# Local transformer layer norm: statistics from token rows on VectorE instead of from features by TensorE

## The chip, the cores and the metric

One core of a Trainium2 chip. The metric is the device time of one execution in microseconds (us), the median of several runs. TensorE does the matmuls and transposes, VectorE, ScalarE and GpSimd the rest, SyncE issues the transfers. In the rows PE is TensorE, PEld its weight loads, DVE is VectorE, ACT is ScalarE, POOL is GpSimd.

## What is computed

Input x is 16 batch rows of 512 tokens by 128 features. The reference, cut:

```python
xn = _layernorm(x)
x = x + _L0_attn_ref(xn, ...) + _L0_ffn_ref(xn, ...)

# _L0_attn_ref: causal attention, 16 heads of 64, with biases
# _L0_ffn_ref: two layers (DEPTH = 2), each:
h = shift_token(x)                       # half of the features come from the token before
q, k, v = jnp.split(h @ wqkv, 3, axis=-1)
q = l2norm(q) * qs; k = l2norm(k) * ksc  # 8 heads of 64
q, k = rotary_xpos(q, k)
x = x + local_attention(q, k, v) @ wo    # windows of 64 tokens, the window before is seen too
h = shift_token(x)
mu = h.mean(-1, keepdims=True); var = h.var(-1, keepdims=True)
h = (h - mu) / jnp.sqrt(var + 1e-05) * lg + lb
a, g = jnp.split(h @ w1 + b1, 2, axis=-1)
x = x + (a * gelu(g)) @ w2 + b2
```

The last formulas, from `mu` to `lb`, and the final sum of the three terms are what the change touches.

## The kernel before

**Work and streams.** All in float32. A batch row passes through 182 steps, each a task such as `("f_wo", l)`: a group of TensorE instructions that fill one or more of 8 PSUM banks, and the instructions on ScalarE or VectorE (sometimes GpSimd too) that read the banks. Steps that begin with `a_` belong to the attention (8 pairs of heads: `a_proj`, `a_v`, `a_max`, `a_neg`, `a_st`, `a_pv`, `a_ot`, `a_out`), steps with `f_` to the local transformer, with the layer (0 or 1) as their first number. A layer has a front (`f_q`, `f_k`, `f_v`, and the transposes `f_qt`, `f_kt`, for 4 token tiles; GpSimd normalises q and k), four rounds of local attention (`f_max`, `f_neg`, `f_st`, `f_pv`, `f_ot`), and a tail: `f_wo`, the layer norm, `f_gate`, three `f_up`, `f_down`. `norm` and `f_first` bring in a batch row, `xt` makes the attention's copy of it, `out` adds everything up and stores.

**What sets the order.** At build time a planner (`least_idle`, L249) walks through four streams at once: layer 0 with `norm` and `f_first`, layer 1, the attention's front, and the attention's rest. It gives every step the costs that stand in the table `STEPS` (L64 to L97), observes the dependences in `needs` (L145) and the 8 banks, keeps the 40 best partial orders after every step, and ranks them by TensorE's idle time in that model plus a penalty when the streams drift apart. The result, `ORDER` (L288), is one list, and every engine works through its own instructions in the order of that list, with semaphore waits for what it needs. So a change of costs in the table moves steps everywhere. Layer 1 of batch row i runs beside layer 0 of batch row i + 1.

**Dependences that matter here.** `f_first` of a batch row needs `f_down` of layer 0 of the row before, `xt` needs `f_first`, and the attention's projections need `xt`; `f_down` of layer 0 needs `f_wo` of layer 1 of the row before; the last `a_out` of a batch row needs `out` of the row before.

**The layer norm before** (features on partitions, tokens along the free axis) takes three steps:
- `f_mean` (L1241, L830): one 128x512 matmul with the matrix `center` subtracts each token's mean; ScalarE copies the result (`centred`) and squares it (`squared`).
- `f_var` (L1245, L984, L703): four matmuls of `squared` with `mean_of` give each token's variance; VectorE adds epsilon (`lvar`), GpSimd takes the power -0.5 (`lrstd`).
- `f_rep` (L1250, L988, L836): four matmuls repeat `lrstd` over the partitions; VectorE scales (`scaled`), ScalarE adds the bias into `lT`, which `f_gate` and `f_up` read.

**The final sum before:** `out` (L1273, L1035) adds `aT` (attention) and `yT` (local transformer) by eight accumulating matmuls with the identity, which also turn them to token rows, and VectorE adds x.

The input norm at the start of each batch row, `token_norm` (L863), works on token rows in SBUF: four `bn_stats`, four `bn_aggr`, an add of epsilon, GpSimd's power, four `tensor_scalar`.

## Time and profile before

| | us |
|---|---|
| median of 3 runs (3051.53 to 3061.63) | 3054.31 |
| span of the profiled execution | 3052.9 |
| TensorE busy | 2932.4 |
| VectorE busy | 1987.4 |
| ScalarE busy | 1704.3 |
| GpSimd busy | 1019.2 |

The profiled execution shows its span, from the first to the last instruction; what lies around the span is not shown separately, and the span is 1.4 us below the median. Busy time counts an engine's instructions; matmuls overlap each other, so a matmul's own duration is longer than the time to the start of the next. A float32 matmul stands as two records, a transpose as one. An idle time in square brackets in a timeline is that of the engine just ahead of the row, with what released it.

### The profile page before, as it was taken

The page shows a single profiled execution, that of the slowest core. Times are in us where ns is not written, and L with a number is a line of the kernel's source. Part 1 is how long each engine was busy: PE and PEld are TensorE (multiplying, and loading weights), DVE is VectorE, ACT ScalarE, POOL GpSimd, SP SyncE. Part 2 cuts the span into 40 slices and gives each one's busy share as a digit, 9 for nine tenths or more (in the row PEclk, how much of TensorE's full clock was granted, in tenths as well). Part 3 has the DMA queues.
Part 4 walks back from the last instruction along what each step waited for, and adds up shares of the span by engine and source line. Part 5 has one row for each costly group of instructions (what it writes and reads, how often), then busy time and mean ns, then how long its engine had stood idle before and what let it go on. Part 6 is the DMA issues. An engine that isn't in the chain of part 4 may idle for free.

```text
span 3052.9 us, 86127 instructions
## 1 busy us (share of the span) xinstructions
PE 2932.4 (96%) x33792; PEld 2004.3 (66%) x33792; DVE 1987.4 (65%) x6942; ACT 1704.3 (56%) x3094; POOL 1019.2 (33%) x1002
## 2 busy tenths in 40 slices
PE   6999999999999999999999999999999999999997
PEld 4666666676666666666666766666667676666764
DVE  5567676666767566676767666676675766666653
ACT  4455464655555565555556655566565655655552
POOL 5134250424324052352414324152250423423230
PEclk9999999999999999999999999999999999999998
DMA  3000000000000000000000000000000000000000
GB/s 102 2 5 2 10 4 2 12 2 12 2 4 10 2 12 2 9 5 2 12 2 9 5 9 5 2 9 5 8 5 2 12 2 8 5 2 9 2 8 5
DMA packets 41783, 25.03 MB, mean 8 GB/s; under 512 B 13058, under 2 KB 40620, under 8 KB 41388
## 3 DMA queue, kind: packets, MB, share of 16 engines
q1 hardware_dynamic: 41388, 19.52, 2.3%
q8 instruction: 277, 4.54, 0.6%
q14 instruction: 118, 0.97, 0.1%
HBM read 14.96 MB, written 4.19 MB: 6 GB/s over the span
## 4 chain that ended last, share of the span: by engine, by line
PE 83%; DVE 7%; ACT 4%; issue 4%; POOL 2%; DMA 0%; POOLq 0%; DVEq 0%; ACTq 0%
PE bank L1139 10%; PE bank L1182 9%; PE bank L1168 7%; PE bank L1056 7%; PE bank L1223 6%; PE bank L1195 4%; PE bank L1239 4%; PE bank L1208 3%; PE bank L1228 3%; PE bank L1049 3%; PE bank L1261 3%; PE bank L1266 3%; PE bank L1050 3%; PE bank L1051 3%; PE bank L1271 2%
## 5 line engine op out<-in xcount | busy, mean ns | idle before, releaser
L910 DVE CUSTOM_DVE_ANT_0 bank<-bank,future 128x128 f32<-128x128 f32 (+3 forms) x1024 | 467.3, 527 | 68.8 <-PE bank L1098 68.2
L925 DVE CUSTOM_DVE_ANT_0 bank<-bank,band 128x192 f32<-128x192 f32 x1024 | 331.0, 394 | 226.1 <-PE bank L1116 225.7
L714 POOL TENSOR_TENSOR rnorm<-ssc,minus_half 128x8 f32<-128x8 f32 x256 | 426.8, 1667 | 21.3
L780 ACT ACTIVATE probs<-bank 128x512 f32<-128x512 f32 (+1 forms) x768 | 346.0, 532 | 143.7 <-PE bank L1148 143.1
L712 POOL TENSOR_SCALAR ssc<-ss 128x8 f32<-128x8 f32 x256 | 99.7, 390 | 934.4 <-DVE ss L970 930.4
L1139 PE MATMUL bank<-Qa,Ka 64*128 64x512 f32 (+3 forms) x2048 | 391.3, 465 | 8.0 <-ACT lprobs L787 4.4
L1182 PEld LDWEIGHTS bank<-Va,probs 128*64 128x64 f32 x10240 | 312.4, 138 | 47.3 <-issue 38.3
L1182 PE MATMUL bank<-Va,probs 128*64 128x65 f32 x10240 | 332.6, 223 | 0.0
L963 DVE TENSOR_TENSOR scratch<-bank,rope_t 128x512 f32<-128x512 f32 x256 | 176.2, 688 | 230.0 <-ACT scratch L807 207.9
L807 ACT ACTIVATE scratch<-bank 128x512 f32<-128x512 f32 x256 | 153.8, 601 | 259.9 <-PE bank L1223 167.5
L787 ACT ACTIVATE lprobs<-bank 128x512 f32<-128x512 f32 x256 | 139.0, 595 | 283.0 <-PE bank L1170 282.9
L1223 PE MATMUL bank<-Lqkv,resid 128*128 128x512 f32 x512 | 272.9, 618 | 4.1 <-ACT resid L800 2.1
L702 POOL TENSOR_TENSOR rstd<-var_eps,minus_half 128x4 f32<-128x4 f32 x16 | 16.1, 1009 | 778.1 <-DVE var_eps L875 778.1
L1168 PE MATMUL bank<-Qf,Kf 64*128 64x64 f32 x4096 | 254.8, 275 | 0.0
L1168 PEld LDWEIGHTS bank<-Qf,Kf 64*128 64x128 f32 x4096 | 240.3, 189 | 15.0
L733 ACT ACTIVATE Qf<-bank 128x512 f32<-128x512 f32 x256 | 152.9, 604 | 91.5 <-PE bank L1056 91.4
L1139 PEld LDWEIGHTS bank<-Qa,Ka 64*128 64x128 f32 x2048 | 158.9, 188 | 37.9 <-issue 26.5
L1195 PEld LDWEIGHTS bank<-V_shifted,lprobs 128*64 128x64 f32 x2048 | 137.0, 138 | 62.8 <-issue 38.1
L970 DVE TENSOR_REDUCE ss<-scratch 128x8 f32<-128x512 f32 x256 | 172.6, 674 | 0.0
L1195 PE MATMUL bank<-V_shifted,lprobs 128*64 128x65 f32 x2048 | 167.3, 228 | 1.0 <-ACT lprobs L787 0.8
L1195 PE MATMUL bank<-Vf,lprobs 128*64 128x65 f32 x2048 | 167.4, 228 | 0.0
L718 POOL TENSOR_TENSOR scratch<-scratch 128x512 f32<-128x512 f32 x128 | 162.8, 1272 | 0.0
(164 smaller groups left out, 6496.5 us busy)
## 6 DMA issues: line engine op xcount, KB each, us to landing
x_res<-in_L_attn_x SPq DMA_DIRECT2D x16, 256.0 KB, 2.9
x_rows<-in_L_attn_x SPq DMA_DIRECT2D x16, 256.0 KB, 3.2
out<-yT SPq DMA_DIRECT2D x16, 256.0 KB, 2.5
Lqkv<-in_L_ffn_wqkv SPq DMA_DIRECT2D x2, 768.0 KB, 4.8
rope_t<-in_rope SPq DMA_DIRECT2D x8, 128.0 KB, 4.7
Kf<-in_L_attn_W_qkv SPq DMA_DIRECT2D x1, 768.0 KB, 7.4
Qf<-in_L_attn_W_qkv SPq DMA_DIRECT2D x1, 768.0 KB, 9.0
Lw<-in_L_ffn_w SPq DMA_DIRECT2D x2, 341.0 KB
```

The costliest lines, as they stand in the source:

```text
L714: g.tensor_tensor(rnorm[s][:, :], ssc[:, :], minus_half[:, :], ALU.pow).then_inc(rnorm_ready.sem, 1)
L780: psum.raise_read(a.activation(probs[j][:, at:at + n], psum.bank(i, task, (u, j))[:, 0:n], ACT.Exp, scale=float(HEAD) ** -0.5), i, task, ( ...
L910: ins = v.tensor_tensor_reduce(psum.bank(i, task, (u, j))[:, at:at + n], psum.bank(i, task, (u, j))[:, at:at + n], future[:, SEQ - n:SEQ], ...
L925: ins = v.tensor_tensor_reduce(psum.bank(i, task, (u, j))[:, k * BAND:(k + 1) * BAND], psum.bank(i, task, (u, j))[:, k * BAND:(k + 1) * BAND],
L963: v.tensor_tensor(heads(turn_a), src, table(0, 0, HEAD), ALU.mult)
L970: v.tensor_reduce(ss[s][:, :], heads(squares), AX.X, ALU.add).then_inc(sums_ready.sem, 1)
L1056: ins = nc.tensor.transpose(bank[:, t * P:(t + 1) * P], src(t), ident[:, :])
L1139: mm(bank[j][:, at:end], Ka[p % 2][HALF[j], tile(k)], Qa[p % 2][HALF[j], queries], start=True, stop=False)
L1168: mm(bank[j][:, queries], K_padded[l][HALF[j], keys], Qf[l][HALF[j], p, queries], start=False, stop=False)
L1182: ins = mm(bank[part, t * (HEAD + 1):(t + 1) * (HEAD + 1)], probs[j][:, at + part.start:at + part.stop], Va[p // 2 % 2][:, k, 2 * (p % 2) ...
L1195: ins = mm(bank[HALF[b % 2], t * (HEAD + 1):(t + 1) * (HEAD + 1)], lprobs[j][:, b * BLOCK:(b + 1) * BLOCK], V[:, t, 2 * p + j, :], start=T ...
L1223: psum.raise_filled(mm(bank[:, :], resid[l][:, tile(t)], Lqkv[l][:, c * INNER:(c + 1) * INNER], start=True, stop=True), i, task, kind[2])
```

## The change

The layer norm is done on token rows. `f_rows` replaces `f_mean` and `f_var`: four TensorE transposes turn the residual (`resid`) into token rows in a bank; VectorE takes `bn_stats`, `bn_aggr` and the add of epsilon, waits for GpSimd's power, and writes centred and scaled rows into `lrows` (part of the buffer `ff`). `f_back` replaces `f_rep`: four transposes turn the rows back, and ScalarE applies gain and bias in one instruction into `lT`. In `out`, VectorE first adds `aT` to `yT`, then TensorE does four transposes in place of eight matmuls. The planner gets new costs, and the constants `center` and `mean_of` go.

```diff
-    "f_var": [("pe", 0.9, (), (0,), ()), ("dve", 0.15, (0,), (), (0,)), ("pool", 0.95, (1,), (), ())],
+    "f_rows": [("pe", 0.46, (), (0,), ()), ("dve", 2.05, (0,), (), ()), ("pool", 1.0, (1,), (), ()), ("dve", 1.4, (2,), (), (0,))],
+    "f_back": [("pe", 0.46, (), (0,), ()), ("act", 0.8, (0,), (), (0,))],
...
@@ -165,7 +164,7 @@
         if at[1]:
             return [(i, ("f_k", at[0], at[1] - 1), 0)]
...
-                elif kind == "f_mean":
-                    j0, t0 = earlier(i, task, lambda t: t[0] == "f_up" and t[2] == LAST_UP)
-                    psum.wait_read(act, j0, t0, "a")
-                    psum.wait_filled(act, i, task, "c")
-                    a.activation(centred, psum.bank(i, task, "c")[:, :], ACT.Copy)
-                    psum.raise_read(a.activation(squared, psum.bank(i, task, "c")[:, :], ACT.Square), i, task, "c")
-                elif kind == "f_rep":
+                elif kind == "f_back":
                     l = task[1]
                     if i == 0:
                         act.wait_ge(params, PARAMS)
                     j0, t0 = earlier(i, task, lambda t: t[0] == "f_up" and t[2] == LAST_UP)
                     psum.wait_filled(act, j0, t0, "a")
-                    psum.wait_read(act, i, task, "r")
-                    a.activation(lT[:, :], scaled, ACT.Identity, bias=lnb[:, l:l + 1]).then_inc(lt_ready.sem, 1)
+                    alone(i, task, "h", lT[:, :], psum.bank(i, task, "h")[:, :], ACT.Identity, scale=lng[:, l:l + 1], bias=lnb[:, l:l + 1])
...
+            def token_stats(i, task, mark):
+
+                bank = tiles_of(psum.bank(i, task, mark)[:, :])
+                j0, t0 = earlier(i, task, lambda t: t[0] == "f_rows")
+                psum.wait_read(dve, j0, t0, "c")
+                psum.wait_filled(dve, i, task, mark)
+                for t in range(TILES):
+                    ins = v.bn_stats(lstats[:, t, :], bank[:, t, :])
+                ins.then_inc(rows_ready.sem, 1)
+                rows_ready.wait(dve, i, task, "s")
+                for t in range(TILES):
+                    ins = v.bn_aggr(lmv[:, t, :], lstats[:, t, :])
+                ins.then_inc(rows_ready.sem, 1)
+                rows_ready.wait(dve, i, task, "a")
+                v.tensor_scalar(lvar[:, :], lmv[:, :, 1], EPS, None, ALU.add).then_inc(rows_ready.sem, 1)
+                j0, t0 = earlier(i, task, lambda t: t[0] == "f_back")
+                psum.wait_filled(dve, j0, t0, "h")
+                rstd_ready.wait(dve, i, task, "p")
+                for t in range(TILES):
+                    ins = v.tensor_scalar(lrows[:, t, :], bank[:, t, :], lmv[:, t, 0:1], lrstd[:, t:t + 1],
+                                          ALU.subtract, ALU.mult)
+                psum.raise_read(ins, i, task, mark)
...
-                elif kind == "f_var":
-                    psum.wait_filled(dve, i, task, "v")
-                    psum.raise_read(v.tensor_scalar(
-                        lvar[:, :], psum.bank(i, task, "v")[:, 0:2 * TILES].rearrange("p (t n) -> p t n", n=2)[:, :, 0],
-                        EPS, None, ALU.add), i, task, "v")
-                elif kind == "f_rep":
-                    l = task[1]
-                    if i == 0:
-                        dve.wait_ge(params, PARAMS)
-                    psum.wait_read(dve, i, ("f_mean", l), "c")
-                    psum.wait_filled(dve, i, task, "r")
-                    psum.raise_read(v.scalar_tensor_tensor(scaled, centred, lng[:, l:l + 1], psum.bank(i, task, "r")[:, :],
-                                                           ALU.mult, ALU.mult), i, task, "r")
+                elif kind == "f_rows":
+                    token_stats(i, task, "c")
...
-                        if p == PAIRS - 1:
-                            psum.wait_filled(dve, before_it(i, task, ("out",)), ("out",), "t")
...
+                    other = ("a_out", PAIRS - 1)
+                    psum.wait_read(dve, before_it(i, task, other), other, "u")
+                    other = ("f_down", DEPTH - 1)
+                    psum.wait_read(dve, i, other, "w")
+                    v.tensor_tensor(yT[:, :], yT[:, :], aT, ALU.add).then_inc(sum_ready.sem, 1)
...
-                elif kind == "f_mean":
+                elif kind == "f_rows":
                     l = task[1]
-                    bank = psum.claim(pe, i, task, "c", [(("f_wo", l), "w")])
-                    psum.raise_filled(mm(bank[:, :], center[:, :], resid[2 * l][:, 0:SEQ], start=True, stop=True), i, task, "c")
-                elif kind == "f_var":
-                    bank = psum.claim(pe, i, task, "v", [(("f_mean", task[1]), "c")])
-                    for t in range(TILES):
-                        ins = mm(bank[:, 2 * t:2 * t + 2], squared[:, tile(t)], mean_of[:, :], start=True, stop=True)
-                    psum.raise_filled(ins, i, task, "v")
-                elif kind == "f_rep":
-                    rstd_ready.wait(pe, i, ("f_var", task[1]), "p")
-                    bank = psum.claim(pe, i, task, "r")
-                    for t in range(TILES):
-                        ins = mm(bank[:, tile(t)], lrstd[:, t:t + 1].broadcast_to([P, P]), ident[:, :], start=True, stop=True)
-                    psum.raise_filled(ins, i, task, "r")
+                    transposes(i, task, "c", lambda t: resid[2 * l][:, tile(t)], [(("f_wo", l), "w")])
+                elif kind == "f_back":
+                    transposes(i, task, "h", lambda t: lrows[:, t, :], [(("f_rows", task[1]), "c")])
...
-                    lt_ready.wait(pe, i, ("f_rep", l), "h")
                     for j, (c, m) in enumerate(HID_CHUNKS):
-                        bank = psum.claim(pe, i, task, j)
+                        bank = psum.claim(pe, i, task, j, [(("f_back", l), "h")])
...
-                    other = ("a_out", PAIRS - 1)
-                    psum.wait_read(pe, before_it(i, task, other), other, "u")
-                    bank = psum.claim(pe, i, task, "t", [(("f_down", DEPTH - 1), "w")])
-                    for t in range(TILES):
-                        mm(bank[:, tile(t)], aT[:, tile(t)], ident[:, :], start=True, stop=False)
-                        ins = mm(bank[:, tile(t)], yT[:, tile(t)], ident[:, :], start=False, stop=True)
-                    psum.raise_filled(ins, i, task, "t")
+                    sum_ready.wait(pe, i, task, "y")
+                    transposes(i, task, "t", lambda t: yT[:, tile(t)])
```

**How the order moves: TensorE, layer 1 of the eighth batch row, from its f_wo on.** `Qf,Lwo` is `f_wo`, `GLU,Lw` is `f_down` of layer 0 of the next batch row, `resid,center` is `f_mean`, `Wqkv` is `a_proj` or `a_v` of the attention, `identb,neg` is `a_neg`. Before:

```order
L1239 MATMUL bank<-Qf,Lwo 128x512 x4
L1271 MATMUL bank<-GLU,Lw 128x512 x3
L1244 MATMUL bank<-resid,center 128x512
L1049 MATMUL bank<-Wqkv_hi,xT_hi 128x256
L1050 MATMUL bank<-Wqkv_hi,xT_lo 128x256
L1051 MATMUL bank<-Wqkv_lo,xT_hi 128x256
L1049 MATMUL bank<-Wqkv_hi,xT_hi 128x256
L1050 MATMUL bank<-Wqkv_hi,xT_lo 128x256
L1051 MATMUL bank<-Wqkv_lo,xT_hi 128x256
L1126 MATMUL bank<-identb,neg 128x128 x4
```

Of the change, from the last `f_ot` of layer 1 on (`ident,resid` is `f_rows`, `ident,ff` is `f_back`, L1255 `f_gate`, L1260 `f_up`, `ident,x_res` is `f_first` and then `xt`):

```order
L1061 MATMUL bank<-ident,Of 128x128 x4
L1244 MATMUL bank<-Qf,Lwo 128x512 x4
L1265 MATMUL bank<-GLU,Lw 128x512 x3
L1061 MATMUL bank<-ident,resid 128x128 x4
L1061 MATMUL bank<-ident,ff 128x128 x4
L1255 MATMUL bank<-lT,Lw 128x512 x2
L1255 MATMUL bank<-lT,Lw 85x512
L1260 MATMUL bank<-lT,Lw 128x512
L1061 MATMUL bank<-ident,x_res 128x128 x4
L1260 MATMUL bank<-lT,Lw 128x512
L1061 MATMUL bank<-ident,x_res 128x128 x4
L1228 MATMUL bank<-Lqkv,resid 128x512 x2
```

Before, 13 rows of attention stood between `f_mean` and `f_var`, of which 7 are shown; now `f_rows` and `f_back` stand next to each other. Such a pair, `ident,resid` with `ident,ff` right behind it, stands at 15 of the 32 layer norms of the changed program: layer 1 of every batch row but the third. In 14 of them `f_wo` and `f_down` stand right ahead as here, in the last batch row `f_wo` alone. In 12 of the batch rows before the last, the twelve steps from `f_st` of the third round to `f_wo` have nothing of another stream among them either; in the program before, the last batch row alone was so. From the seventh batch row on the order of the change repeats itself, up to the last two.

**VectorE at the same place.** Before (L980 and L981 are `f_wo`, L1016 and L1017 `f_down`, then `norm` of a later batch row, L985 `f_var`, L994 `f_rep`):

```order
L980 TENSOR_TENSOR resid<-bank,resid 64x512
L981 TENSOR_TENSOR resid<-bank,resid 64x512
L1016 SCALAR_TENSOR_TENSOR resid<-bank,b2s,resid 64x512
L1017 SCALAR_TENSOR_TENSOR resid<-bank,b2s,resid 64x512
L868 BN_STATS stats<-x_res 128x6 x4
L872 BN_AGGR mv<-stats 128x2 x4
L875 TENSOR_SCALAR var_eps<-mv 128x4
L878 TENSOR_SCALAR x_res<-x_res,mv,rstd 128x128 x4
L985 TENSOR_SCALAR lvar<-bank 128x4
L994 SCALAR_TENSOR_TENSOR ff<-ff,lng,bank 128x512
```

Of the change (L993 and L994 are `f_wo`, L1018 and L1019 `f_down`, L879 to L891 `f_rows`):

```order
L993 TENSOR_TENSOR resid<-bank,resid 64x512
L994 TENSOR_TENSOR resid<-bank,resid 64x512
L1018 SCALAR_TENSOR_TENSOR resid<-bank,b2s,resid 64x512
L1019 SCALAR_TENSOR_TENSOR resid<-bank,b2s,resid 64x512
L879 BN_STATS lstats<-bank 128x6 x4
L883 BN_AGGR lmv<-lstats 128x2 x4
L886 TENSOR_SCALAR lvar<-lmv 128x4
L891 TENSOR_SCALAR ff<-bank,lmv,lrstd 128x128 x4
L858 BN_STATS stats<-x_res 128x6 x4
L862 BN_AGGR mv<-stats 128x2 x4
L865 TENSOR_SCALAR var_eps<-mv 128x4
L868 TENSOR_SCALAR x_res<-x_res,mv,rstd 128x128 x4
```

The four rows of `f_rows` come behind the adds of `f_wo` and `f_down`, and `norm` behind them.

**TensorE behind the out of the last batch row but one.** Before, layer 1 of the last batch row begins so (`Lqkv` is `f_q`, `f_k` or `f_v`; `qn` and `kn` are `f_qt` and `f_kt`; L1208, L1098 and L1182 are attention):

```order
L1223 MATMUL bank<-Lqkv,resid 128x512
L1098 MATMUL bank<-Ka,Qa 128x128 x2
L1098 MATMUL bank<-Ka,Qa 128x256 x2
L1098 MATMUL bank<-Ka,Qa 128x384 x2
L1098 MATMUL bank<-Ka,Qa 128x512 x2
L1182 MATMUL bank<-Va,probs 64x65 x20
L1228 MATMUL bank<-Lqkv,resid 128x512
L1223 MATMUL bank<-Lqkv,resid 128x512
L1056 MATMUL bank<-ident,qn 128x128 x4
L1223 MATMUL bank<-Lqkv,resid 128x512
L1182 MATMUL bank<-Va,probs 64x65 x20
L1056 MATMUL bank<-ident,kn 128x128 x4
```

Of the change (`ident,yT` is `out`, L1213 the last `a_out`):

```order
L1260 MATMUL bank<-lT,Lw 128x512 x2
L1260 MATMUL bank<-lT,Lw 85x512
L1265 MATMUL bank<-GLU,Lw 128x512 x3
L1061 MATMUL bank<-ident,yT 128x128 x4
L1213 MATMUL bank<-OaT,Wout 128x512
L1228 MATMUL bank<-Lqkv,resid 128x512 x2
L1233 MATMUL bank<-Lqkv,resid 128x512
L1228 MATMUL bank<-Lqkv,resid 128x512
L1061 MATMUL bank<-ident,qn 128x128 x4
L1228 MATMUL bank<-Lqkv,resid 128x512
L1061 MATMUL bank<-ident,kn 128x128 x4
L1233 MATMUL bank<-Lqkv,resid 128x512
```

The attention of the last batch row is over before this layer begins, and the rest of the program has rows of layer 1 alone; before, the attention ran beside it up to the second round.

## Rows read from the trace of the kernel before

**Rows 1.** Page, part 1: busy time of each engine
```profile
PE 2932.4 (96%) x33792; PEld 2004.3 (66%) x33792; DVE 1987.4 (65%) x6942; ACT 1704.3 (56%) x3094; POOL 1019.2 (33%) x1002
```

**Rows 2.** Windows: middle and last stretch; busy us (x instructions) per engine, PEclk, DMA share, GB/s
```profile
200.00:2800.00 2600.00, 2537.16 (x29320) 1733.59 (x29319) 1736.35 (x6059) 1486.09 (x2697) 903.65 (x853) 1.00 0.02 6
...
2950.00:3053.00 103.00, 81.99 (x886) 53.80 (x882) 45.50 (x152) 37.88 (x70) 24.24 (x23) 0.90 0.01 4
```

**Rows 3.** TensorE timeline, one layer norm in mid-run: start us, us, engine line op
```profile
1237.92 1.02 PE L1244 MATMUL bank<-resid,center 128*128 128x512 f32 x2
1238.87 1.13 PE L1139 MATMUL bank<-Qa,Ka 64*128 64x512 f32 x4
...
1242.17 1.05 PE L1248 MATMUL bank<-mean_of,ff 128*128 128x2 f32 x8
1243.08 0.63 PE L1056 MATMUL bank<-ident,Oa 128*128 128x128 f32 x4
...
1244.32 0.66 PE L1056 MATMUL bank<-ident,x_res 128*128 128x128 f32 x4
1244.81 1.02 PE L1208 MATMUL bank<-OaT,Wout 128*128 128x512 f32 x2
1245.67 1.05 PE L1254 MATMUL bank<-ident,lrstd 128*128 128x128 f32 x8
1246.56 1.88 PE L1223 MATMUL bank<-Lqkv,resid 128*128 128x512 f32 x4
```

**Rows 4.** TensorE timeline, final step out of the last batch row
```profile
3047.62 0.39 PE L1279 MATMUL bank<-ident,yT 128*128 128x128 f32 x2
...
3048.96 0.39 PE L1279 MATMUL bank<-ident,yT 128*128 128x128 f32 x2
```

**Rows 5.** Timeline of VectorE and GpSimd: f_down, norm and f_var in one stretch
```profile
2712.67 0.74 DVE L1016 SCALAR_TENSOR_TENSOR resid<-bank,b2s,resid 64x512 f32<-64x512 f32 x1 [1.25 <-PE bank L1271]
...
2714.22 0.87 DVE L868 BATCH_NORM_STATS2 stats<-x_res 128x6 f32<-128x128 f32 x4
...
2715.79 1.02 POOL L702 TENSOR_TENSOR rstd<-var_eps,minus_half 128x4 f32<-128x4 f32 x1 [56.72 <-DVE var_eps L875]
...
2716.85 1.11 DVE L878 TENSOR_SCALAR x_res<-x_res,mv,rstd 128x128 f32<-128x128 f32 x4 [1.13 <-POOL rstd L702]
...
2717.99 0.16 DVE L985 TENSOR_SCALAR lvar<-bank 128x4 f32<-128x4 f32 x1
```

**Rows 6.** TensorE timeline, end of layer 1 of the last batch row
```profile
3011.10 0.38 PE L1126 MATMUL bank<-identb,negf 128*128 128x128 bf16 x4 [1.52 <-issue]
...
3015.43 0.27 PE L1195 MATMUL bank<-V_shifted,lprobs 128*64 128x65 f32 x1 [0.16 <-ACT lprobs L787]
...
3017.67 0.65 PE L1056 MATMUL bank<-ident,Of 128*128 128x128 f32 x4 [1.07 <-DVE Of L944]
3019.01 3.70 PE L1239 MATMUL bank<-Qf,Lwo 128*128 128x512 f32 x8 [0.69 <-ACT Qf L733]
```

**Rows 7.** TensorE timeline, a_proj, the row behind it, and both a_pv
```profile
1852.11 0.48 PE L1049 MATMUL bank<-xT_hi,Wqkv_hi 128*128 128x512 f32 x1
...
1853.59 1.02 PE L1208 MATMUL bank<-OaT,Wout 128*128 128x512 f32 x2
...
1856.28 2.55 PE L1182 MATMUL bank<-Va,probs 128*64 128x65 f32 x80
```

**Rows 8.** GpSimd timeline, one q and k pair of a front
```profile
1267.14 0.54 POOL L712 TENSOR_SCALAR ssc<-ss 128x8 f32<-128x8 f32 x1 [6.57 <-DVE ss L970]
...
1274.04 1.04 POOL L723 TENSOR_TENSOR kn<-scratch,rnorm 128x512 f32<-128x512 f32 x1 [0.17 <-POOL scratch L718]
```

**Rows 9.** TensorE timeline: one wait of TensorE in mid-run
```profile
1863.46 0.38 PE L1126 MATMUL bank<-identb,neg 128*128 128x128 bf16 x4 [2.46 <-DVE neg L910]
```

**Rows 10.** Windows behind that wait and behind one in the first batch row
```profile
1865.20:1868.60 3.40, 3.40 (x24) 1.73 (x21) 1.00 (x2) 1.08 (x2) 3.21 (x3) 0.50 0.26 77
...
124.40:131.20 6.80, 6.80 (x71) 5.83 (x70) 0.77 (x3) 1.59 (x3) 0.00 (x0) 0.50 0.01 2
```

38 lines of the change are left out of this document (17 added, 21 removed).

## The prediction

> **What bounds the kernel now.** I read the busy times first, then windows, then the waits of TensorE in a timeline. TensorE is busy for 2932.4 of 3052.9 us, VectorE for 65% [rows 1]. In the 2600 us of the middle TensorE is busy for 2537.2 us and its clock stays at full rate [rows 2]: 62.8 us idle, or 4.3 us in each batch row of some 178 us (2600 us hold 14.6 of them). So before the change TensorE's own work sets the time, and the order hides nearly every dependence behind another stream's work. Only where one stream runs alone do the waits show: the last 103 us hold 21.0 us of idle time and a mean clock of 0.90 [rows 2].
>
> So there are two questions: how much work TensorE loses, and whether the new order still hides the chain through VectorE, GpSimd and ScalarE. The second one decides, and it can be read from the order.
>
> **A. TensorE's work: -77 us.** What a step occupies is the time from its start to the next step's start when nothing waits. `f_mean` takes 1238.87 - 1237.92 = 0.95 us, `f_var` 0.91, `f_rep` 0.89, four transposes 0.49 (1244.32 to 1244.81) [rows 3]. A layer norm took 2.75 us and takes 2 x 0.49 = 0.98: 1.77 us less, 32 times, 56.6 us. In `out`, the records of one kind start 0.22 us apart, from 3047.62 to 3048.96 in six steps [rows 4], so its eight matmuls take 8 x 0.22 = 1.79 us; four transposes take 0.49. That is 1.3 us less, 16 times, 20.8 us. Sum 77.4 us, 4.8 us in each batch row. If everything else stayed hidden, this would be the gain.
>
> **B. The hole between f_rows and f_back: +77 us.** In the new order these two stand next to each other on TensorE in layer 1 of 15 batch rows, in 14 of them right behind `f_wo` and `f_down`. TensorE works in order, so it stands still until VectorE has written the rows. VectorE at that time has to add `f_down` and then do the whole of `f_rows`. The parts stand in a row in the trace: from the first add of `f_down`, which starts when its matmuls end, over the input norm with its `bn_stats`, its wait for GpSimd's 1.02 us and its four `tensor_scalar`, from 2712.67 to 2716.85 + 1.11 = 2717.96, 5.29 us; the norm alone takes 3.74 (2714.22 to 2717.96) [rows 5]. `f_rows` is the same instructions on the same shapes, read from a bank in place of SBUF. The adds of `f_wo` run under the matmuls of `f_down`. Of the 5.29 us TensorE covers 0.49 with the transposes of `f_rows`; 4.8 us stay. Then `f_gate` needs the rows turned back: transposes, one 128x512 read by ScalarE, a matmul. The same form stands between the last `f_ot` and `f_wo`, and TensorE waited 0.69 us there [rows 6]. So 4.8 + 0.7 = 5.5 us, 14 times, 77 us. Behind that `norm` stands on VectorE (3.7 us) and `f_first` waits for it, but `f_back`, that wait, `f_gate` and an `f_up` lie between on TensorE, and these are more than 3.7 us. Below: the hole can be no shorter than VectorE's own 3.74 us less 0.49, which gives 4.0 with the 0.7, so 55 us; above: 0.5 us more if reading a bank is slower, 84 us.
>
> **C. Bare rounds ahead of it: +41 us.** In 12 batch rows the last two rounds of layer 1 have no other stream's steps among them. The last batch row ran the same twelve steps bare already before the change, and TensorE waited there 1.52 us ahead of `f_neg`, 0.16 ahead of `f_pv`, 1.07 ahead of `f_ot`, 0.69 ahead of `f_wo` [rows 6]: 3.44 us, 12 times, 41 us.
>
> **D. The clock: +24 us.** The clock fell to half rate, 1.2 GHz, for 3.4 us right behind a wait of 2.46 us in mid-run [rows 9, 10], and for 6.8 us behind waits in the first batch row [rows 10]. TensorE was busy throughout in both stretches, so they cost half: 1.7 and 3.4 us. A hole of 4.8 us, with the 0.7 behind it, is more than twice the wait that brought one on. I take the shorter stretch, since part of it passes in the hole itself: 14 x 1.7 = 24 us. The ends are none and 14 x 3.4 = 48 us. The Trainium skill (TensorE: Matmul & The Clock Gate, section PE-mode transpose) has a rule that speaks against this change: transposes do not count as work for the clock as matmuls do, and all that is left of the layer norm on TensorE is transposes, on both sides of the hole. By that rule the longer stretch would be the common one, and the sum 24 us higher. No row here shows transposes alone, so the sum stays with the mid-run row.
>
> **E. The end of the program: +26 us.** The attention of the last batch row is now over before its layer 1 begins. Its front then goes at the pace of GpSimd: a q and k pair takes 1267.14 to 1275.08, 7.94 us [rows 8], four pairs 31.8 us. TensorE has 12 matmuls of 0.94 (half of 1.88) and 8 transposes of 0.49 in it [rows 3], 15.2 us, so 16.6 us idle. Entering and leaving that stretch through ScalarE and VectorE I put at 4 us, with 0 and 8 as ends. Two more rounds are bare, 2 x 3.4. The `out` ahead of it waits for two adds of `f_down` and one of the sum on VectorE, about 3 us more than it did. Against this, some 5 of the 21.0 us of idle time at the end [rows 2] lay in the mixed stretch that is gone. 16.6 + 4 + 6.9 + 3 - 5 = 26 us. The very last layer norm has a shorter chain than its three steps had, and the last `out` a longer one; I put both together at nothing.
>
> **F. Edits that cost nothing.** In layer 0, `f_rows` and `f_back` have other work between them: two transposes steps (`a_ot`, `f_kt`), one `a_proj` of 1.48 us (1852.11 to 1853.59), both `a_pv` 2.55 [rows 7], one `a_out` 0.86 [rows 3], together 5.9 us against the 3.74 that VectorE needs. Without that cover it would be B once more. VectorE gains some 90 us of work over the whole run (3.74 less the wait for GpSimd and less the one small and one 128x512 instruction removed, 32 times, and 16 adds); it is at 65%, and this sits in its idle time except where B counts it. ScalarE loses instructions. The small idle time of mid-run stays, but the tenth of it that lay where B and C now are goes: -6 us.
>
> **Sum.** -77 + 77 + 41 + 24 + 26 - 6 = +85. The profiled span of 3052.9 becomes 3138, and with the 1.4 us by which the median lies above it, **3139 us, 2.8% slower**.
>
> **The rivals.**
> 1. *The bound engine's saving comes through*, 3054 - 77 = **2977 us**. For it: TensorE is at 96%, a whole batch row of other work exists, and the three old steps waited on each other too and hardly showed. Against it: the order of the change. Its one point of decision is the exposed time in a batch row, which has to stay below the 4.8 us saved; B and C give 5.5 + 3.4. Chance 0.08. The Trainium skill (Perfetto Trace Analysis, section Identifying the Most-Contended Engine) says to optimize the engine with the highest occupancy first, and this is what comes out by that rule.
> 2. *VectorE held up by GpSimd in layer 0.* The power for `lrstd` stands in GpSimd's queue behind the q and k work, and VectorE now waits for it with everything behind. The cover has 5.9 - 3.7 = 2.2 us to spare; half a pair (4 us [rows 8]) ahead of it would expose about 2 us, and the stopped VectorE would delay the reads of `a_pv`. 16 times 2.3 us, **3176 us**. Against it: three more steps of attention stand between the last `f_k` and `f_rows`. Chance 0.12.
> 3. *Half of B and C is hidden and the clock stays up*, because the new order is tighter elsewhere and mid-run idle time halves: 3139 - 59 - 24 = 3056, or less by up to 31 us: around **3050 us**. Against it: TensorE issues in order, so nothing later can fill the hole. Chance 0.08.
>
> My forecast keeps 0.72. **The numbers.** About 0.3%, 9 us, is what a measurement of this kernel can tell from no change. Faster takes rival 1 and a third of rival 3: 0.10; the same, half of rival 3: 0.04; slower, the rest: 0.86. Below, the range takes the forecast without the clock's cost and with mid-run idle time halved, 3139 - 24 - 31 = 3084; above, the longer clock stretches, 3163, and rival 2 with most of them, 3190.
>
> **What would show it.** Right: TensorE's busy time falls, and its busy share falls from 96% to about 90%; in each batch row a wait of nearly 5 us ahead of the transposes of `ff` (L1061), released by VectorE's `tensor_scalar` (L891); windows at half clock right behind it; a front of layer 1 at the end that takes over 30 us with GpSimd busy throughout; 15 layer norms of the 32 with a hole. Wrong: if those transposes wait less than 2 us, B fails and rival 1 is near; if the clock never falls in mid-run, D; if waits gather ahead of the layer 0 `f_back`, rival 2.

## The result and the profile after

| | before | change |
|---|---|---|
| median, us | 3052.92 | 3285.98 |
| lowest to highest, us | 3050.92 to 3061.63 | 3284.43 to 3287.63 |
| span of the profiled execution, us | 3052.9 | 3282.6 |

The change is slower by a ratio of 1.0756 [1.0740, 1.0771]: 233 us where the forecast had 85, and outside its range. The direction was right, and the holes stand where the forecast put them, as the trace shows. The cost of the clock and idle time elsewhere were put far too low.

The page of the changed kernel, part 1, busy time of each engine:

```profile
PE 2964.1 (90%) x33280; PEld 1994.8 (61%) x33280; DVE 2065.6 (63%) x7310; ACT 1689.3 (51%) x3030; POOL 1019.3 (31%) x999
```

TensorE has 512 matmul records fewer than in [rows 1] and is busy for 31.7 us longer. The windows answer to those of [rows 2], and two are added: one steady batch row, and the two stretches of it at half clock (busy us and instructions of PE, PEld, DVE, ACT, POOL, then the clock):

```profile
200.00:2800.00 2600.00, 2386.74 (x27057) 1607.35 (x27056) 1677.95 (x5943) 1375.52 (x2470) 828.47 (x781) 0.97 0.02 6
...
1733.00:1934.40 201.40, 184.10 (x2080) 124.02 (x2079) 128.48 (x456) 105.57 (x189) 62.59 (x59) 0.97 0.02 6
...
1721.70:1728.40 6.70, 6.59 (x70) 5.54 (x67) 0.71 (x3) 1.58 (x3) 0.00 (x0) 0.50 0.00 0
1742.20:1748.90 6.70, 5.47 (x9) 2.43 (x10) 2.69 (x14) 2.96 (x4) 1.01 (x1) 0.50 0.00 1
...
3150.00:3283.00 133.00, 89.11 (x470) 51.32 (x470) 48.10 (x146) 33.65 (x54) 30.75 (x29) 0.65 0.02 7
```

In mid-run the clock is no longer 1.00. In the steady part it falls twice in every batch row, for some 6.8 us each time, and the last 133 us of the program have a mean clock of 0.65. Summed over the run, the clock stands at half rate, 1.2 GHz, for 272.8 us in 32 stretches, against 36.1 us in 6 before (both counts take in some 2 us behind the last instruction).

The waits of TensorE, grouped by what ended them (us in total, times, longest; `issue` means that the profile shows nothing it waited for), first of the change:

```profile
PE bank L1061 <- DVE ff L891: 81.1, 17, 5.7
PE bank L1131 <- issue: 25.8, 26, 2.5
PE bank L1255 <- ACT lT L729: 19.0, 29, 0.9
PE bank L1061 <- DVE yT L1040: 18.2, 14, 2.5
PE bank L1103 <- ACT Qa L729: 18.1, 11, 1.7
PE bank L1103 <- ACT probs L776: 15.0, 28, 0.7
...
PE bank L1144 <- ACT lprobs L783: 13.2, 12, 1.1
PE bank L1061 <- DVE Of L957: 12.6, 14, 1.1
```

and those of before that answer to them (L1056 was the transposes' line, L1126 that of `f_neg` and `a_neg`):

```profile
PE bank L1126 <- issue: 6.6, 13, 1.5
...
PE bank L1056 <- DVE Of L944: 4.4, 6, 1.1
PE bank L1139 <- ACT lprobs L787: 4.4, 4, 1.1
...
PE bank L1098 <- ACT probs L780: 3.1, 9, 0.5
...
PE bank L1261 <- ACT lT L843: 2.8, 4, 1.7
PE bank L1098 <- ACT Qa L733: 2.2, 2, 1.4
```

**Where 230 us of span come from.** TensorE's idle time rose from 120.5 to 318.5 us, by 198. Its busy time rose by 31.7 although its work at full clock fell by the 77 of term A, so some 109 us are left over for half clock. The records of the clock allow that: 272.8 - 36.1 = 236.7 us more at half rate cost at most half of that, 118. Then -77 + 198 + 109 = 230. What is left over takes in every other error, that of term A too. Read directly, half of the time that TensorE is busy inside the recorded stretches is 217.5 / 2 = 108.7 us of the change and 28.7 / 2 = 14.3 before, so 94 us more; the other 15 are not accounted for. By place, the 108.7 are 38 around the 14 holes of mid-run, 32 in ten stretches in the bare rounds, 31 from the `out` of the last batch row but one on (before: 7) and 7 elsewhere.

One steady batch row shows it too. It takes 201.4 us. Before, by an estimate, it took 2932.4 / 16 = 183.3 us of busy time at the busy share of mid-run, 0.976, so 187.8. Of the 13.6 us between them, -4.8 are saved work, 17.3 - 4.5 = +12.8 idle time, and the rest, +5.6, the clock; half of the busy time in its two stretches is (6.59 + 5.47) / 2 = 6.0.

The place is the one forecast. TensorE's timeline at the end of layer 1 of a batch row in mid-run (start, us, engine, line, then in brackets the wait ahead of it):

```profile
1720.04 0.38 PE L1131 MATMUL bank<-identb,negf 128*128 128x128 bf16 x4 [1.53 <-issue]
...
1721.43 3.45 PE L1173 MATMUL bank<-Qf,Kf 64*128 64x64 f32 x32
...
1729.10 0.66 PE L1061 MATMUL bank<-ident,Of 128*128 128x128 f32 x4 [0.81 <-DVE Of L957]
1730.44 3.70 PE L1244 MATMUL bank<-Qf,Lwo 128*128 128x512 f32 x8 [0.69 <-ACT Qf L729]
1733.98 2.74 PE L1265 MATMUL bank<-GLU,Lw 128*128 128x512 f32 x6
1736.56 0.60 PE L1061 MATMUL bank<-ident,resid 128*128 128x128 f32 x4
1742.50 1.11 PE L1061 MATMUL bank<-ident,ff 128*128 128x128 f32 x4 [5.34 <-DVE ff L891]
1744.54 2.93 PE L1255 MATMUL bank<-lT,Lw 128*128 128x512 f32 x3 [0.93 <-ACT lT L729]
```

and VectorE's timeline of the same hole:

```profile
1736.83 0.74 DVE L1018 SCALAR_TENSOR_TENSOR resid<-bank,b2s,resid 64x512 f32<-64x512 f32 x1 [1.25 <-PE bank L1265]
...
1741.08 1.37 DVE L891 TENSOR_SCALAR ff<-bank,lmv,lrstd 128x128 f32<-128x128 f32 x4 [1.19 <-POOL lrstd L701]
```

The hole of term B is there, 5.34 + 0.93 us, and so are the waits of term C, 1.53, 0.81 and 0.69. What the forecast had not seen is the second stretch at half clock: it begins at 1721.7, right behind the wait of 1.53 us, and the 32 matmuls of L1173 take 3.45 us, where a round at full clock took 1.98.

### The profile page after: what moved, and what is told of

It reads as the page before. It is cut to its first block, busy times and chain, and to the rows that moved or that the text cites. A ratio compares the mean times of both kernels' runs of the same rounds, so it can differ in the third digit from the quotient of the medians.

```text
span 3282.6 us, 85395 instructions
## 1 busy us (share of the span) xinstructions
PE 2964.1 (90%) x33280; PEld 1994.8 (61%) x33280; DVE 2065.6 (63%) x7310; ACT 1689.3 (51%) x3030; POOL 1019.3 (31%) x999
## 4 chain that ended last, share of the span: by engine, by line
PE 74%; DVE 11%; ACT 6%; issue 6%; POOL 2%; DMA 0%; ACTq 0%; DVEq 0%; POOLq 0%
PE bank L1187 9%; PE bank L1061 8%; PE bank L1144 8%; PE bank L1173 7%; PE bank L1228 6%; PE bank L1200 4%; PE bank L1213 3%; PE bank L1244 3%; PE bank L1255 3%; DVE bank L923 3%; PE bank L1233 3%; PE bank L1054 2%; PE bank L1131 2%; PE bank L1056 2%; PE bank L1055 2%
## 5 line engine op out<-in xcount | busy, mean ns | idle before, releaser
L1144 PE MATMUL bank<-Qa,Ka 64*128 64x512 f32 (+3 forms) x2048 | 389.5, 462 | 18.2 <-ACT lprobs L783 13.2
L701 POOL TENSOR_TENSOR lrstd<-lvar,minus_half 128x4 f32<-128x4 f32 x32 | 32.5, 1014 | 947.6 <-DVE lvar L886 947.5
L1228 PE MATMUL bank<-Lqkv,resid 128*128 128x512 f32 x512 | 279.5, 632 | 4.9 <-ACT resid L796 2.8
L1173 PE MATMUL bank<-Qf,Kf 64*128 64x64 f32 x4096 | 274.5, 288 | 0.0
L1173 PEld LDWEIGHTS bank<-Qf,Kf 64*128 64x128 f32 x4096 | 259.5, 202 | 15.9 <-issue 1.4
L1200 PE MATMUL bank<-V_shifted,lprobs 128*64 128x65 f32 x2048 | 176.7, 236 | 3.1 <-ACT lprobs L783 2.4
L1200 PE MATMUL bank<-Vf,lprobs 128*64 128x65 f32 x2048 | 177.0, 236 | 0.0
L1200 PEld LDWEIGHTS bank<-V_shifted,lprobs 128*64 128x64 f32 x2048 | 146.7, 146 | 47.6 <-issue 24.1
```

The costliest lines, as they stand in the source:

```text
L1144: mm(bank[j][:, at:end], Ka[p % 2][HALF[j], tile(k)], Qa[p % 2][HALF[j], queries], start=True, stop=False)
L1173: mm(bank[j][:, queries], K_padded[l][HALF[j], keys], Qf[l][HALF[j], p, queries], start=False, stop=False)
L1200: ins = mm(bank[HALF[b % 2], t * (HEAD + 1):(t + 1) * (HEAD + 1)], lprobs[j][:, b * BLOCK:(b + 1) * BLOCK], V[:, t, 2 * p + j, :], start=T ...
L1228: psum.raise_filled(mm(bank[:, :], resid[l][:, tile(t)], Lqkv[l][:, c * INNER:(c + 1) * INNER], start=True, stop=True), i, task, kind[2])
```

## The experiments

Two theories. **Order:** the edits by themselves save the 77 us, and the planner's new order, which leaves layer 1 bare, loses them and more. **Steps:** the new steps themselves put VectorE between two pieces of TensorE's work and are slower in any order. Beside them stands a question of size: how much is the clock, and how much the waits.

### The edits in the order of before

The planner is given the costs of before, and its finished order is then renamed:

```diff
+ORDER = [(i, ({"f_mean": "f_rows", "f_rep": "f_back"}.get(t[0], t[0]), *t[1:])) for i, t in ORDER if t[0] != "f_var"]
```

> All edits of the change, but every step stands in the order of the kernel before: f_rows in the place of f_mean, f_back in the place of f_rep, f_var left out. Theory 1, the new order is what costs (it leaves the chain of layer 1 bare): TensorE's saving of some 77 us comes through for the most part, 2975 to 3010 us. Theory 2, the new layer norm itself costs, since VectorE is held for 5 us in one piece and waits for GpSimd with everything behind it, in whatever order: 3070 to 3150 us, with waits for VectorE's rows at most of the 32 layer norms.

Measured: 3243.63 us, ratio 1.0603 [1.0582, 1.0623]. That is above the ranges of both theories. So the order of before doesn't carry the new steps either, and the theory of the order alone is wrong in its simple form. The waits of TensorE show why (L894 is the line of the scaled rows here, L1043 that of the sum in `out`):

```profile
PE bank L1064 <- DVE yT L1043: 65.9, 16, 7.3
PE bank L1057 <- DVE ff L894: 37.9, 8, 5.6
PE bank L1147 <- DVE ff L894: 22.6, 5, 5.5
PE bank L1106 <- DVE ff L894: 17.7, 5, 5.9
```

The sum in `out` costs 0.69 us on VectorE, yet TensorE waits up to 7.3 us for it. VectorE's timeline ahead of one of them:

```profile
1349.02 0.29 DVE L926 CUSTOM_DVE_ANT_0 bank<-bank,future 128x128 f32<-128x128 f32 x1
...
1354.43 0.69 DVE L991 TENSOR_TENSOR scratch<-scratch 128x512 f32<-128x512 f32 x1
1355.03 0.69 DVE L1043 TENSOR_TENSOR yT<-yT,aT 128x512 f32<-128x512 f32 x1
```

Instructions of other steps, without a gap from 1349.02 to 1355.03, stand ahead of the sum in VectorE's queue. Its own inputs had been ready since 1346.72 (1345.96 + 0.76). TensorE waited 5.27 us for it, up to 1355.77. In this order TensorE runs ahead of VectorE by those steps. With the old steps that hardly showed: TensorE was idle for 120.5 us in all, against 310.4 here.

### The steps of before in the order of the change

```diff
+ORDER = [(i, (kind, *t[1:])) for i, t in ORDER
+         for kind in {"f_rows": ("f_mean", "f_var"), "f_back": ("f_rep",)}.get(t[0], (t[0],))]
```

> The steps of the kernel before (old layer norm and old out, nothing of the change's edits), in the order that the planner made for the change: f_mean and f_var in the place of f_rows, f_rep in the place of f_back. Theory 1, the order costs: the holes stay, since the old chain has four waits of 1.2 to 1.7 us when nothing covers it (5.8 us in all, against 5.3 + 0.9 of the new one), and TensorE's 77 us of work come back: 3330 to 3370 us. Theory 2: the old steps do not mind the order, 3060 to 3150 us.

Measured: 3372.54 us, 1.1018 [1.0990, 1.1045], just above the range of the first theory. The order is bad for the old steps too, and as bad: TensorE is idle for 317.8 us (a span of 3372.8 less 3055.0 busy), against 318.5 with the new steps, and what differs is its busy time, by 90.9 us. In the order of the change the edits are thus worth 3372.54 - 3285.98 = 87 us in their favour, and in the order of before they cost 3243.63 - 3055.46 = 188 us. A price of the edits without an order does not exist.

### The hole filled with matmuls

Right ahead of `f_back`, where it follows `f_rows` directly, five matmuls are written into its bank, which the transposes then overwrite. They need nothing from VectorE, so the hole keeps its length but TensorE is not idle in it.

```diff
+                    bank = psum.claim(pe, i, task, "h")
+                    if PLACE[i, task] == PLACE[i, ("f_rows", task[1])] + 1:
+                        for _ in range(FILLERS):
+                            mm(bank[:, :], Wout[:, 0, :], resid[2 * task[1]][:, 0:SEQ], start=True, stop=True)
```

> The changed kernel with five extra 128x512 matmuls (results overwritten, the output stays as it is) ahead of f_back wherever it stands right behind f_rows, 4.7 us of work in a hole of 5.3. If half clock behind the hole costs about 2.5 us each time, as I now read the trace (6.8 us at half rate in each batch row there): 35 us less than the change, 3245 to 3260 us, and only one stretch at half clock in a batch row in mid-run. If the clock costs nothing there: 3286 to 3295 us.

Measured: 3242.19 us, 1.0597 [1.0572, 1.0621], 44 us less than the change. The wait for `ff` falls from 81.1 us to 16.0, since the fillers stand in it, and half clock falls from 272.8 us to 150.9 (20 stretches). TensorE does 75 matmuls more and the program is faster, so idle time in the hole does bring the clock down: around the 14 holes of mid-run the change had 14 stretches of 6.8 us, and here four of 3.4 us are left, each some 8 us behind the first filler of a hole.

The gain is not 44 / 15 at each hole, though. Out of the profiled execution (3246.8 us, the slowest of four), the stretch ahead of the hole and one whole batch row:

```profile
1706.90:1720.50 13.60, 12.10 (x72) 7.59 (x71) 1.21 (x4) 2.19 (x4) 0.00 (x0) 0.50 0.00 0
1523.00:1724.40 201.40, 188.55 (x2092) 125.61 (x2091) 128.54 (x457) 105.61 (x189) 62.58 (x59) 0.97 0.02 6
```

In four batch rows in a row the stretch that began in the bare rounds became twice as long, 13.7 us, and these rows take 201.4 us as they did unfilled. There the loss moved and did not go. Of the 38 us by which this execution's span is shorter than that of the change, none comes from these four rows, some 10 from the time behind the `out` of the last batch row but one, and the rest from the rows before and behind the four.

### The bare rounds filled too

The same, with one matmul more ahead of each `f_neg` of the last two rounds of layer 1 that has three steps of the local transformer right ahead of it, 15 in all. The expectation speaks of one ahead of `f_wo` too; the kernel that ran has none there.

```diff
+                    if kind == "f_neg" and task[1:] in ((1, 3), (1, 2)) and all(t[0][0] == "f" for _, t in ORDER[PLACE[i, task] - 3:PLACE[i, task]]):
+                        bank = psum.claim(pe, i, task, "m")
+                        mm(bank[:, :], Wout[:, 0, :], resid[2][:, 0:SEQ], start=True, stop=True)
```

> As fill_hole (3242 us), with one more 128x512 matmul ahead of the bare f_neg of the fourth round and a 128x256 one ahead of the f_wo behind it, in each batch row with bare rounds. The first stretch at half clock in a batch row (6.8 us, it slows f_st from 2.0 to 3.5 us) begins behind the wait of 1.5 us at that f_neg. If that wait alone sets it off: it goes in some 12 batch rows, 12 x 2 to 3 us, 3205 to 3220 us. If the waits behind it would bring it on as well: 3235 to 3250 us.

Measured: 3228.91 us, 1.0568 [1.0549, 1.0587]; 13 us less than with the hole alone filled, between the two ranges expected. Half clock falls to 85.8 us in 17 stretches. A steady batch row takes 197.9 us in place of 201.4, with one stretch of 3.4 us, which now begins at `f_wo`, behind the waits of 1.07 and 0.69 us that stayed unfilled. TensorE's waits elsewhere stay: 19.0 us for `lT`, 18.1 for `Qa`, 18.0 for `yT`. Together the fillers give back 57 us. The clock's loss itself, counted as above, falls by more, from 108.7 to 33.7 us. Part of what it gives back goes into longer waits (for `Of` 15.0 us in place of 12.6, for `lprobs` in `f_pv` 4.4 in place of 2.4); the rest is not traced.

### The order of before, with norm behind f_rows

In the order of before, `norm` stands ahead of `f_rows` of layer 1 and so ahead of it in VectorE's queue, with its wait for GpSimd. The two are exchanged:

```diff
+for k in range(1, len(ORDER) - 1):
+    if ORDER[k][1][0] == "norm" and ORDER[k + 1][1] == ("f_rows", 1):
+        ORDER[k], ORDER[k + 1] = ORDER[k + 1], ORDER[k]
```

> As new_in_old_order (3244 us), with one edit: where norm stands right ahead of f_rows of layer 1, the two change places, so that VectorE does the layer norm's rows before the next input's. Theory 3: in the old order the new layer norm is late because VectorE has 3.7 us of norm to do first (it hardly mattered for the old one, whose only VectorE work there was one 0.16 us instruction), so the waits for its rows (95 us in all there) lose about 3.5 us at each of 14 to 16 places: 3170 to 3200 us. If VectorE's queue is not the cause but the length of the chain itself: 3235 to 3250 us.

Measured: 3221.44 us, 1.0547 [1.0528, 1.0566]: 22 us less than without the exchange, between the two ranges expected. Waits of TensorE in this run (L1046 is the sum in `out`, L874 the input norm, L897 the rows):

```profile
PE bank L1067 <- DVE yT L1046: 65.9, 16, 7.3
PE bank L1067 <- DVE x_res L874: 29.0, 12, 7.5
PE bank L1060 <- DVE ff L897: 15.4, 8, 3.4
```

The largest group of waits for the rows fell from 37.9 to 15.4 us, all waits for them together from 106.5 to 57.8. The wait for the input norm, which now comes later, rose from 7.8 us (2 times) to 29.0 (12 times). So VectorE's queue is a part of the cause, and the exchange moves a good part of the wait from one step to the other.

### The new layer norm with the old out

In the order of before, with `out` as it was (eight accumulating matmuls, no sum on VectorE):

```diff
-                    v.tensor_tensor(yT[:, :], yT[:, :], aT, ALU.add).then_inc(sum_ready.sem, 1)
...
-                    transposes(i, task, "t", lambda t: yT[:, tile(t)])
+                    for t in range(TILES):
+                        mm(bank[:, tile(t)], aT[:, tile(t)], ident[:, :], start=True, stop=False)
+                        ins = mm(bank[:, tile(t)], yT[:, tile(t)], ident[:, :], start=False, stop=True)
```

> As new_in_old_order, with the out step of the kernel before (eight matmuls on TensorE instead of VectorE's sum and four transposes). There TensorE waited 66 us in all for VectorE's sum, 4.1 us at each of 16 out steps. If those waits come from VectorE's queue ahead of the sum: they go, TensorE has 21 us more work, and about 15 us of half clock go with them: 3175 to 3205 us. If something else would make TensorE wait there anyway: 3240 to 3265 us.

Measured: 3179.59 us, 1.0406 [1.0388, 1.0424], 64 us less. So of the 188 us that the edits cost in the order of before, `out` makes 64 and the layer norm 124 (from 3055.46 to 3179.59). The edit of `out` saves TensorE 1.3 us and makes it wait 4.1 (65.9 / 16).

### The planner set to other offsets

Two runs leave the change as it is and alter only the planner's arguments: how many partial orders it keeps, how far each stream is meant to lag, and how strongly it is held to that. No step is moved by hand.

```diff
-ORDER = least_idle(40, (0.0, 1.4, 1.1, 1.2), 0.2, 0.05)
+ORDER = least_idle(40, (0.0, 1.5, 0.7, 0.8), 0.2, 0.05)
```

> The changed kernel with another setting of the planner (offsets of the streams 1.5, 0.7, 0.8 in place of 1.4, 1.1, 1.2), nothing else: another order of the same steps. Theory 1: the time follows the order, and with fewer bare layer norms it comes down to 3090 to 3180 us. Theory 2: the time stays within 1% of the change, 3255 to 3320 us, whatever the order.

Measured: 3087.79 us, 1.0095 [1.0074, 1.0116], at the lower end of what the order theory expected; 198 us less than the change by one tuple of numbers. Half clock falls to 60.5 us in 6 stretches, TensorE is busy for 2873.3 us.

```diff
-ORDER = least_idle(40, (0.0, 1.4, 1.1, 1.2), 0.2, 0.05)
+ORDER = least_idle(60, (0.0, 1.3, 0.9, 1.2), 0.4, 0.1)
```

> The changed kernel with the planner's setting that came out best of some 450 by its own model (60 orders kept in place of 40, offsets 1.3, 0.9, 1.2, spread 0.4, weight 0.1), nothing else. In its order no layer norm but the very last has f_rows and f_back side by side. Theory 1 (the order costs, the edits save 77 us of TensorE's work where they are covered): 2975 to 3010 us, below the kernel before. If VectorE's longer piece with its wait for GpSimd costs in any order: 3050 to 3100 us, as with the first other setting (3088).

Measured: **2986.91 us, 0.9778 [0.9758, 0.9798]**, faster than both kernels. Its page, part 1, and the window that answers to [rows 2]:

```profile
PE 2859.4 (96%) x33280; PEld 1937.3 (65%) x33280; DVE 2063.5 (69%) x7310; ACT 1676.5 (56%) x3030; POOL 1019.9 (34%) x999
```

```profile
200.00:2800.00 2600.00, 2536.42 (x29678) 1721.82 (x29677) 1846.73 (x6573) 1494.17 (x2703) 913.05 (x861) 1.00 0.02 6
```

TensorE is idle as little as before the change, at full clock, and has done more of the program in the same 2600 us (29678 matmul records, and the change needs fewer in all). Its waits for the rows:

```profile
PE bank L1061 <- DVE ff L891: 9.8, 8, 4.2
```

9.8 us in place of 81.1. The steps are those of the change, word for word, so they can be hidden; the theory that they are slower in any order falls.

### The steps of before with that same setting

> The kernel before, unedited but for the planner's setting of new_searched (60 orders kept, offsets 1.3, 0.9, 1.2, spread 0.4, weight 0.1). Theory 1 has two halves. If the gain of new_searched (2987 us, 67 us below the kernel before) is all from the edits, the old steps stay at 3045 to 3060 us. If it is in good part the better order, the old steps gain from it as well: 2990 to 3020 us, and the edits themselves are worth only the rest, 5 to 35 us of the 77 that TensorE saves.

The diff is that line of the planner's arguments alone, in the kernel before. Measured: 3016.33 us, 0.9870 [0.9851, 0.9889]. So at this setting 38 us of the gain come to the old steps as well, and 3016.33 - 2986.91 = 29 us come from the edits. The setting was chosen for the new steps. No run has the old steps at a setting chosen for them, so the 29 us hold for this setting, and the edits' worth between the best orders of both is not shown. Its page, part 1:

```profile
PE 2931.6 (97%) x33792; PEld 2000.4 (66%) x33792; DVE 1993.4 (66%) x6942; ACT 1707.8 (57%) x3094; POOL 1019.1 (34%) x1002
```

TensorE's busy time differs by 2931.6 - 2859.4 = 72.2 us between the two, with 13 us more at half clock for the new steps (37.2 against 24.3), which cost at most 6. That bears out term A, 77 us. Idle time takes 45 us of it back: 2984.9 - 2859.4 = 125.5 against 3011.6 - 2931.6 = 80.0.

### The last front filled

At the end of the program, two or three matmuls ahead of each transposing step of the last front, 20 in all, in the idle time that GpSimd leaves there:

```diff
+                    if (i, task[1]) == (BATCH - 1, 1):
+                        bank = psum.claim(pe, i, task, c)
+                        for _ in range(2 if c == "q" else 3):
+                            mm(bank[:, :], resid[1][:, tile(0)], Lqkv[1][:, 0:INNER], start=True, stop=True)
```

> The changed kernel with 20 extra 128x512 matmuls in the front of layer 1 of the last batch row (two ahead of each f_qt, three ahead of each f_kt, overwritten by the transposes), where TensorE waits for GpSimd. There the clock falls to half and stays there for 65 us, through all four rounds behind it (f_st 3.65 us in place of 1.98). If it stays low because the front left TensorE half idle: the rounds run at full clock, 6.6 in place of 9.4 us each, and the end of the program is 12 to 25 us shorter, 3261 to 3274 us. If the bare rounds keep the clock down by themselves: 3283 to 3295 us.

Measured: 3284.3 us, 1.0744 [1.0719, 1.0769]; no gain. Windows of this run, in the front and in the rounds behind it:

```profile
3190.00:3208.00 18.00, 14.54 (x44) 6.29 (x42) 7.04 (x15) 6.99 (x13) 14.85 (x14) 1.00 0.00 0
3211.00:3225.00 14.00, 10.85 (x110) 8.91 (x112) 4.72 (x26) 3.56 (x5) 0.00 (x0) 0.50 0.00 1
3225.00:3250.00 25.00, 22.79 (x233) 18.48 (x232) 8.63 (x44) 6.15 (x11) 0.00 (x0) 0.53 0.01 2
```

and TensorE's timeline between them:

```profile
3207.08 0.66 PE L1061 MATMUL bank<-ident,kn 128*128 128x128 f32 x4 [1.28 <-POOL kn L719]
3208.74 0.21 PE L1119 MATMUL bank<-Kf,Qf 64*128 64x64 bf16 x2 [1.00 <-issue]
...
3211.96 0.59 PE L1131 MATMUL bank<-identb,negf 128*128 128x128 bf16 x4 [2.70 <-issue]
3213.30 0.61 PE L1166 MATMUL bank<-ahead,row_of 64*128 64x512 bf16 x2 [0.75 <-ACT negfT L768]
...
3213.77 3.65 PE L1173 MATMUL bank<-Qf,Kf 64*128 64x64 f32 x32
```

The fillers did what they were for: the front ran at full clock (1.00 in place of 0.50). But GpSimd sets its pace, so nothing came of it, and the clock fell behind the front all the same, at 3211.0, in the chain that enters the first round, with waits of 1.28, 1.00, 2.70 and 0.75 us. So a front at half clock is not needed for slow rounds.

## Why the prediction was right or wrong

| term | forecast, us | measured, us |
|---|---|---|
| A, work of TensorE | -77 | -77 taken; -72 between the two kernels at the last setting |
| idle time: B, C, E and F | 77 + 41 + 26 - 6 = 138 | 198 |
| of it waits like those of B | 77 | 97: `ff` 81.1, `lT` 19.0 - 2.8 |
| of it waits like those of C | 41 | 33: issue 19.2, `Of` 8.2, `Qf` 5.9 |
| of it waits that no term named | -6 | 65: `Qa`, `probs`, `lprobs`, `Qf` at L1131, `yT` |
| D, clock | 24 | 109 left over, 94 read directly |
| sum, with 109 | 85 | 230 |

The measured waits are differences over the whole run, so those of the end lie within them. Alone, the end had 133 - 89.1 = 43.9 us of idle time where it had 21.0, 23 more against the 26 of E.

**A was right**, as far as the two kernels at the last setting show it. The row distances of [rows 3] and [rows 4] gave it.

**B was right in mechanism and place, a little small.** The hole is 5.34 + 0.93 us in place of 4.8 + 0.7. From the first add of `f_down` to the end of the rows VectorE takes 5.62 us (1736.83 to 1741.08 + 1.37) where the forecast had 5.29. Of the difference `tensor_scalar` brings 0.26: from a bank it takes 1.37 us for the four, from SBUF 1.11 [rows 5]. Its bound for that, 0.5 us, holds, but 14 x 6.27 = 88 us lie above its upper end for B, 84.

**C was near**, 33 us for 41, but the forecast took it for the whole price of the bare rounds. Behind its first wait, of 1.53 us, the clock fell too.

**The steps that failed are D and the idle time outside B, C and E.** Of the 145 us between forecast and span, D is 85 and idle time 60.

D reads: "I take the shorter stretch, since part of it passes in the hole itself: 14 x 1.7 = 24 us." Two things were wrong. All 14 stretches around the holes were the longer one, 6.8 us, and cost 2.7 us each (half of the 5.5 for which TensorE is busy in one): 38 us in place of 24. And D had no term for two other places: the bare rounds, where ten stretches cost 32 us, and the end. In mid-run D looked only at the wait of 2.46 us of [rows 9]. Yet the stretch in the first batch row of [rows 10], from 124.4 on, stands behind this wait of the kernel before:

```profile
122.81 0.38 PE L1126 MATMUL bank<-identb,negf 128*128 128x128 bf16 x4 [1.52 <-issue]
```

It is the very wait that C counts, so the trace of before already showed a bare round with a stretch of 6.8 us behind it. That idle time is the cause, and not only a neighbour, is shown by the fillers: 44 us came back with the hole filled, 13 more with the rounds filled, although in four batch rows the first moved the loss and did not lessen it. The upper end of D, 14 x 3.4 = 48 us, would have covered the holes alone. The rule of the Trainium skill (TensorE: Matmul & The Clock Gate, section PE-mode transpose), by which transposes don't count as work for the clock and the sum would have been 24 us higher, gave the right length of these stretches. No run here tests its reason: the four transposes of `resid` at 1736.56 still ran at full rate (0.60 us), those of `ff` behind the hole at half (1.11 us). It doesn't explain the other stretch, which begins among the matmuls of a bare round.

**The rest of D is at the end.** The window of the last 103 us had a clock of 0.90, which is about 21 us at half rate; that of the last 133 us has 0.65, about 93 us. By the direct count the clock cost 31 us from the `out` of the last batch row but one on, where before it cost 7. E counted waits there and no clock. One bare round takes 9.36 us (L1173 from 3213.28 to 3222.64) where it took 6.65 before (3005.84 to 3012.49), and there are four of them.

**Idle time of 65 us stood in no term.** TensorE waits 15.9 us more for `Qa`, 11.9 for `probs`, 8.8 for `lprobs`, 10.0 for `Qf` at L1131 and 18.2 for `yT` (the new `out`, whose longer chain the forecast looked at in the last batch row alone). The forecast had put this at -6: it took the idle time of mid-run for a constant per batch row, which holds only as long as the order does. Probably the steps of the attention that had stood in the bare stretches now stand closer to each other elsewhere, and there their own chains show. That is argued from the lines; no run moved these waits alone, and their cause is not shown. A batch row before was also 187.8 us and not 178, which changed no term by more than 1 us.

**The rivals.** Rival 1, 2977 us, did not come with this order. With an order that fits the edits the time is near it, 2986.91, but 38 us of that the old steps gain as well, so that is not its saving of 77 coming through. The sentence of the Trainium skill that was named there (Perfetto Trace Analysis, section Identifying the Most-Contended Engine), to optimize the engine with the highest occupancy first, is borne out at that setting, by 29 us, and not by the change as it stands. (For TensorE the page wants the share of its weight loads looked at; with 66% beside VectorE's 65% [rows 1] it points at the same engine, but only just.) Rival 2 did not come: no wait ahead of the `f_back` of layer 0 stands among the larger ones, and 81.1 us in 17 waits for `ff` leave next to nothing for 16 more. Rival 3 did not come: idle time elsewhere rose, and the clock fell.

**Of the signs named,** the share of 90%, the waits of about 5 us ahead of the transposes of `ff`, the half clock behind them and the front of over 30 us all came. The busy time of TensorE did not fall but rose, by 31.7 us, a sign that D was too small.

## What to carry to other kernels

Work taken from the engine that sets the time is worth its duration only if the order can be made anew around it: here the same edits gave +188 us in the old order, +233 in the planner's first new one beside the old kernel, and -29 at a setting searched for them, beside the old steps at that same setting. So search the order with the change before judging it, and search it for the old version too, which was not done here. A step moved to an engine with time to spare still stands in that engine's queue: what counts is not its 0.69 us but the 6 us of other work ahead of it when the bound engine needs the answer. And where one engine holds the clock, price each newly exposed wait at its length and again for a slow stretch behind it, here some 2.7 to 3.4 us where one came. Filling one wait can move that stretch to the next, so judge fillers by the time of whole batch rows.

## What the runs showed of the hardware that was not expected

- A wait's length alone doesn't tell what the clock does. Ahead of `f_neg` in a bare round TensorE waits 1.52 or 1.53 us. In eight steady batch rows of the change, 6.8 us at half clock follow, and before the change they followed in the first batch row. In the last one [rows 6] they did not, and the clock stayed at 1.00 (last window below). Nor do they follow in an earlier batch row of the change itself, here with the wait, the 32 matmuls of the round in 1.98 us and the window:

```profile
1319.97 0.38 PE L1131 MATMUL bank<-identb,negf 128*128 128x128 bf16 x4 [1.53 <-issue]
...
1321.36 1.98 PE L1173 MATMUL bank<-Qf,Kf 64*128 64x64 f32 x32
```

```profile
1320.30:1328.00 7.70, 5.66 (x97) 4.53 (x96) 1.96 (x7) 2.77 (x5) 0.00 (x0) 1.00 0.00 0
```

- Half clock held on through work that kept TensorE busy. With the last front filled, the rounds from 3225 to 3250 ran at 0.53 with TensorE busy for 22.79 of 25 us; before the change, the same rounds ran at full clock with TensorE busy for only 9.12 of 12 us, as this window of the kernel before shows:

```profile
3006.00:3018.00 12.00, 9.12 (x163) 7.56 (x161) 5.14 (x25) 3.75 (x7) 0.00 (x0) 1.00 0.01 2
```

  The rounds entered low stayed low, and those entered at full rate stayed there. What sets this apart is left open.
- Adding 75 matmuls to the engine that sets the time made the kernel 44 us faster, and in some batch rows not at all.
